# A two-block transformer kernel: the first attention's exponentials read their scores head by head from PSUM, norm offsets move to GpSimd, pair starts are loaded at once, and the work gets a new order

## The reference, cut to what matters

```python
x = x + xattn0(layernorm(x), ctx)     # 16 heads of 16 features, softmax over 77 keys
x = x + ffn0(layernorm(x))            # 256 -> 1024, relu, 1024 -> 256, add its input, layernorm again
x = x + xattn1(layernorm(x), ctx)     # one head; both sides normed
x = x + ffn1(layernorm(x))            # each position takes one of 8 256x256 matrices

scores = einsum('bqhd,bkhd->bhqk', q, k) / 4
weights = softmax(scores, axis=-1)
out = einsum('bhqk,bkhd->bqhd', weights, v)
```

## Time and profile before

| | |
|---|---|
| median of 3 runs | 317.99 us (317.55 to 318.81) |
| span of the profiled execution, first to last instruction | 314.0 us |
| what the runs have around that span (median minus span) | 4.0 us |
| PE busy | 267.9 us (85%) |
| PEld busy | 232.0 us (74%) |
| VectorE busy | 254.8 us (81%) |
| ScalarE busy | 181.7 us (58%) |
| GpSimd busy | 157.3 us (50%) |
| mean granted TensorE clock | 0.932 of full speed |

### The profile page before, as it was taken

The page is one execution under the profiler, slowest core; times in us unless marked ns, Lnnn a source line. Parts: engine busy times, 40 slices in busy tenths (PEclk is TensorE's granted clock), DMA queues, the critical chain, the costliest instruction groups (busy, mean ns, idle before and its releaser), DMA issues.

```text
span 314.0 us, 6283 instructions
## 1 busy us (share of the span) xinstructions
PE 267.9 (85%) x2080; PEld 232.0 (74%) x2080; DVE 254.8 (81%) x664; ACT 181.7 (58%) x606; POOL 157.3 (50%) x157
## 2 busy tenths in 40 slices
PE   2954958977999998999999989999989999878960
PEld 2743937763999698689789959988878988666850
DVE  2998998972889999998997789899899986875640
ACT  2468628526368857478695857775754471454510
POOL 2253640275225878821652263268766653164854
PEclk9995596995999999999999999999999999997995
DMA  6922010240000372100001000011110000000222
GB/s 177 336 72 77 8 42 25 67 142 27 3 0 3 115 222 51 29 24 2 2 0 35 2 0 2 33 52 51 37 36 0 2 0 1 3 0 34 87 78 73
DMA packets 8797, 15.32 MB, mean 49 GB/s; under 512 B 1270, under 2 KB 6813, under 8 KB 8509
## 3 DMA queue, kind: packets, MB, share of 16 engines
q1 hardware_dynamic: 6845, 9.68, 9.2%
q0 software_dynamic: 1920, 5.25, 5.9%
HBM read 11.77 MB, written 3.15 MB: 48 GB/s over the span
## 4 chain that ended last, share of the span: by engine, by line
PE 37%; DVE 29%; issue 15%; POOL 12%; ACT 3%; DVEq 1%; DMA 1%; POOLq 0%; SPq 0%; ACTq 0%
PE PB L256 16%; PE PB L249 7%; PE PB L460 5%; DVE SM L598 3%; POOL SM L1220 3%; DVE SX L649 3%; DVE SM L609 3%; PE S L365 3%; PE S L377 2%; POOL out_x L1282 2%; DVE WD L837 2%; PE PB L327 2%; POOL RAW L1275 2%; DVE XN L701 2%; POOL HL L1254 2%
## 5 line engine op out<-in xcount | busy, mean ns | idle before, releaser
L1220 POOL TENSOR_TENSOR SM<-SM,nhalf 128x2 f32<-128x2 f32 x40 | 29.4, 737 | 98.4 <-DVE SM L604 97.9
L1060 ACT ACTIVATE E<-S,SX 128x77 f32<-128x77 f32 x128 | 39.5, 340 | 16.8 <-DVE SX L652 16.6
L256 PE MATMUL PB<-XTH,W1H 128*128 128x256 f32 x128 | 38.3, 299 | 3.9 <-issue 2.2
L1254 POOL TENSOR_TENSOR HL<-HF,HH 128x512 fp32r<-128x512 f32 x26 | 34.5, 1335 | 13.6 <-DVE HH L682 12.0
L1094 ACT ACTIVATE HF<-PB,cols 128x256 f32<-128x256 f32 x64 | 26.8, 473 | 20.9 <-PE PB L256 20.6
L256 PE MATMUL PB<-W2H,HH 128*128 128x256 f32 x128 | 37.9, 296 | 1.1 <-DVE HL L688 1.1
L256 PE MATMUL PB<-XTH,W1L 128*128 128x256 f32 x128 | 36.4, 284 | 0.0
L256 PE MATMUL PB<-XTL,W1H 128*128 128x256 f32 x128 | 36.4, 284 | 0.0
L256 PE MATMUL PB<-W2H,HL 128*128 128x256 f32 x128 | 35.8, 280 | 0.0
L256 PE MATMUL PB<-W2L,HH 128*128 128x256 f32 x128 | 35.8, 279 | 0.0
L460 PE MATMUL PB<-WD,XP 128*128 x120 | 29.9, 402 | 0.8 <-issue 0.8
(11 more groups left out here) (188 smaller groups left out, 778.3 us busy)
## 6 DMA issues: line engine op xcount, KB each, us to landing
RAW<-in_w SPq DMA_DIRECT2D x4, 512.0 KB, 5.0
WD<-in_WD SPq DMA_DIRECT2D x2, 1024.0 KB
X<-in_x SPq DMA_DIRECT2D x4, 256.0 KB, 7.1
x<-X SPq DMA_DIRECT2D x4, 256.0 KB, 2.2
bc<-in_rows SPq DMA_DIRECT2D x1, 768.0 KB, 7.3
RAW<-in_w_q SPq DMA_DIRECT2D x1, 256.0 KB, 4.2
Wo<-in_w_o SPq DMA_DIRECT2D x1, 256.0 KB, 7.8
RAW<-in_WqT SPq DMA_DIRECT2D x1, 256.0 KB
```

Source lines behind the costliest of these rows:

```text
L256: t = e.matmul(dst, a, b, start=first and j == 0, stop=last and j == n - 1)
L1060: t = e.activation(Ei[:, h * NK:(h + 1) * NK], P[:, at:at + NK], ACT.Exp, bias=SX[:, i, 2, k:k + 1], accum_out=SX[:, i, 1, k:k + 1])
L1220: e.tensor_tensor(sm(K, g, 9), sm(K, g, 8), nhalf[:, :], ALU.pow).then_inc(s["rs" + K], 1)
L1254: e.tensor_tensor(HL[:, hs, :], HF[:, (4 * g + j) % 3, :, :], f(HH[:, hs, :]), ALU.subtract).then_inc(s["hlP"], 1)
```

## The change

- Every `(g, i, a)` of the first attention now takes the by-head path: 8 exponentials from PSUM with sums. The subtraction, the sum and the separate negation on VectorE are gone; the maximum is written negated (`negate=True`) by the reduction itself. The PSUM area is let go when the exponentials are done, in all cases. `smax` now waits for the exponentials of the group before instead of for its transposes, and `ssum` for its `rr`.
- `rs` on GpSimd makes, besides the inverse root, -mean (a product with a tile of -1) and -mean/deviation, in two more instructions of 128x2 with a wait between; line 609 on VectorE is gone.
- The 15 beginnings are read in one call on each of PE, VectorE and ScalarE (`starts()`), at a fixed place in the middle of the first attention.
- The lists of all four engines are written anew. Stage C of groups 0 to 4 comes later (`cs(0)` now stands behind `w1(4, ...)` and before `w1(5, ...)` on PE), `q` and `sc` of group 0 earlier.

The diff, cut to its core (the new lists are told by the rows below and by two of their lines):

```diff
+        minus = sb("minus", [128, 2])
...
+        def load_starts(e, row, most, at):
+
+            values = nc.values_load_multi_w_load_instructions(EV[0:1, row, 0:NP], engines=[e.engine],
+                                                              min_val=0, max_val=most)[1]
+            for n in range(NP):
+                at[n] = values[n]
...
-                P = hold(("sc", g, i, a), ("S", k), ("ex", n + 1) if by_head(i, a) else ("sub", n // 2 + 1))
+                P = hold(("sc", g, i, a), ("S", k), ("ex", n + 1))
...
+            def starts():
+                w.wait_ge(s["route2"], 1)
+                load_starts(e, 0, 7 * 256, start)
...
-                    if n not in start:
-                        start[n] = e.value_load(EV[0:1, 0, n:n + 1], min_val=0, max_val=7 * 256)
...
-                e.scalar_tensor_tensor(out=sm(K, g, 10), in0=sm(K, g, 6), scalar=-1.0, in1=sm(K, g, 9),
-                                       op0=ALU.mult, op1=ALU.mult).then_inc(s["mr" + K], 1)
...
             def smax(g, i, a):
-                n, sv, mx_, hs = scores(g, i, a)
                 w.wait_ge(s["sc"], n + 1)
                 if g:
+                    w.wait_ge(s["ex"], n - 3)
+                e.tensor_reduce(two(SX[:, i, 0, 8 * a:8 * a + 8]), sv, AX, ALU.max, negate=True).then_inc(s["mx"], 1)
+
+            def ssum(g, i, a):
+                n, hs = 4 * g + 2 * i + a, slice(8 * a, 8 * a + 8)
+                w.wait_ge(s["ex"], n + 1)
+                if g:
                     w.wait_ge(s["rr"], n - 3)
-                    w.wait_ge(s["tE"], n - 3)
-                step(e.tensor_reduce(mx_, sv, AX, ALU.max))
-                settle()
-                if by_head(i, a):
-                    e.tensor_scalar(SX[:, i, 2, hs], SX[:, i, 0, hs], -1.0, None, ALU.mult).then_inc(s["neg"], 1)
-                else:
-                    e.tensor_tensor(E[:, i, a, 0:8 * NK].rearrange("p (u h k) -> p u h k", u=2, h=4), sv,
-                                    mx_.unsqueeze(3).to_broadcast([128, 2, 4, NK]),
-                                    ALU.subtract).then_inc(s["sub"], 1)
...
                 e.reciprocal(SX[:, i, 2, hs], SX[:, i, 1, hs]).then_inc(s["rc"], 1)
...
-                if by_head(i, a):
-                    P = bank("sc", g, i, a)
-                    w.wait_ge(s["neg"], n // 2 + 1)
-                    if g:
-                        w.wait_ge(s["tE"], n - 3)
-                    for h in range(8):
...
-                else:
-                    w.wait_ge(s["sub"], n // 2 + 1)
-                    t = e.activation(Ei, Ei, ACT.Exp)
+                P = bank("sc", g, i, a)
+                w.wait_ge(s["mx"], n + 1)
+                if g:
+                    w.wait_ge(s["tE"], n - 3)
+                for h in range(8):
+                    at = h // 4 * 512 + h % 4 * NK
+                    k = 8 * a + h
+                    t = e.activation(E[:, i, a, h * NK:(h + 1) * NK], P[:, at:at + NK], ACT.Exp,
+                                     bias=SX[:, i, 0, k:k + 1], accum_out=SX[:, i, 1, k:k + 1])
...
                 e.tensor_tensor(sm(K, g, 9), sm(K, g, 8), nhalf[:, :], ALU.pow).then_inc(s["rs" + K], 1)
+                if K != "Y":
+                    e.tensor_tensor(sm(K, g, 11), sm(K, g, 6), minus[:, :], ALU.mult).then_inc(s["nm"], 1)
+                    minus_made[0] += 1
+                    w.wait_ge(s["rs" + K], g + 1)
+                    w.wait_ge(s["nm"], minus_made[0])
+                    e.tensor_tensor(sm(K, g, 10), sm(K, g, 11), sm(K, g, 9), ALU.mult).then_inc(s["mr" + K], 1)
...
+            w2(6, 1, 0); tB(7, 2); w2(6, 1, 1); tC(5, 0); cp(4, 1); w1(7, 0, 2); w1(7, 1, 0); cs(5, 2); w1(7, 2, 3)
+            tD(0, 0); co(4); w1(7, 3, 3); pr(0, 0, 0); tD(1, 3); pr(0, 1, 1); w2(7, 0, 0, 3); w2(7, 0, 1); tD(2, 2)
```

More of the change, by code:

```diff
@@ L378, in tE, with pv @@
                 t.then_inc(s["tE"], 1)
-            def pv(g, a, p):
+            def pv(g, a, p=None):
                 w.wait_ge(s["vb"], g // 4 + 1)
                 w.wait_ge(s["et"], 4 * g + 2 + a + 1)
-                P = hold(("pv", g), ("B", p), ("o", g + 1)) if a == 0 else PB[p]
+                P = hold(("pv", g), ("B", p), ("o", g + 1)) if a == 0 else PB[place["pv", g][1]]
                 for c in range(2):
@@ L416, in w2 @@
                     hl_here(w, g, j)
-                P = hold(("w2", g), ("B", p), ("y", g + 1)) if i + h == 0 else PB[p]
+                P = hold(("w2", g), ("B", p), ("y", g + 1)) if i + h == 0 else PB[place["w2", g][1]]
                 ts = slice(i * 128, (i + 1) * 128)
@@ L572, in setup @@
                 step(e.memset(nhalf[:, :], -0.5))
+                step(e.memset(minus[:, :], -1.0))
                 step(e.memset(E[:, :, :, 8 * NK:5 * CW], 0.0))
@@ L737, in vector, with starts @@
             begin = {}
+            def starts():
+                w.wait_ge(s["route2"], 1)
+                load_starts(e, 1, 7 * 256, begin)
             def pa(b, r):
@@ new lines, in vector @@
+            stats("C", 2); ssum(5, 0, 0); hh(3, 0); smax(5, 0, 1); hh(3, 2); ssum(5, 0, 1); o(4); hh(3, 3)
+            smax(5, 1, 0); smax(5, 1, 1); ql(7); x1(4); stats("B", 4); ssum(5, 1, 0); apply("B", 4); ssum(5, 1, 1)
+            lo("B", 4); y(3); stats("Y", 3); o(5); x2(3); hh(4, 0); x1(5); stats("B", 5); apply("B", 5); hh(4, 2)
+            smax(6, 0, 0); hh(4, 3); lo("B", 5); smax(6, 0, 1); apply("C", 1); f_o(); ssum(6, 0, 0); cm(0)
+            ssum(6, 0, 1); stats("C", 3); smax(6, 1, 0); smax(6, 1, 1); cm(1); apply("C", 2); x3_(0); ssum(6, 1, 0)
@@ new lines, in vector @@
+            ssum(6, 1, 1); hh(5, 0); hh(5, 2); y(4); stats("Y", 4); hh(5, 3); o(6); smax(7, 0, 0); smax(7, 0, 1)
+            x2(4); cm(2); ssum(7, 0, 0); apply("C", 3); smax(7, 1, 0); ssum(7, 0, 1); x1(6); smax(7, 1, 1)
+            stats("C", 4); x3_(1); stats("B", 6); y(5); apply("B", 6); stats("Y", 5); ssum(7, 1, 0); ssum(7, 1, 1)
+            lo("B", 6); x3_(2); cm(3); x2(5); hh(6, 0); apply("C", 4); hlD(6, 1); x3_(3); hh(6, 2); stats("C", 5)
+            hh(6, 3); o(7); hlD(6, 3); cm(4); x1(7); stats("B", 7); apply("B", 7); apply("C", 5); stats("D", 0)
@@ L996, in scalar @@
+            apply("D", 7); pa(1, 0); pa(1, 1); pa(1, 2); pa(1, 3); pa(1, 4); pa(1, 5); pa(1, 6); pa(1, 7)
         def scalar(e):
@@ new lines, in scalar @@
+            ex(0, 0, 0); hi("A", 1); ex(0, 0, 1); ex(0, 1, 0); rr(0, 0, 0); rr(0, 0, 1); qh(1); ex(0, 1, 1)
+            rr(0, 1, 0); et(0, 0, 0); apply("A", 2); et(0, 0, 1); w_hi(3); et(0, 1, 0); rr(0, 1, 1); w_hi(4)
+            ex(1, 0, 0); et(0, 1, 1); hi("A", 2); apply("A", 3); ex(1, 0, 1); ex(1, 1, 0); rr(1, 0, 0); rr(1, 0, 1)
+            qh(2); et(1, 0, 0); rr(1, 1, 0); f_ct(); hi("A", 3); et(1, 0, 1); apply("B", 0); hi("B", 0); ex(1, 1, 1)
+            ex(2, 0, 0); hf(0, 0); hf(0, 1); apply("A", 4); rr(1, 1, 1); qh(3); et(1, 1, 0); hf(0, 2); et(1, 1, 1)
@@ L1177, in gpsimd @@
+            pc(0, 7); xtc(7); cpt(6); apply("D", 4); cex(7); apply("D", 5); xtd(4); cpt(7); pc(1, 0); xtd(5); pc(1, 1)
+            apply("D", 6); xtd(6); pc(1, 2); apply("D", 7); xtd(7); pc(1, 3); pc(1, 4); pc(1, 5); pc(1, 6); pc(1, 7)
         def gpsimd(e):
```

236 lines of the change are left out of this document (96 added, 140 removed).

## The result

The changed kernel takes 299.75 us (median of 4 runs, 297.38 to 301.69), the one before 317.77 beside it (4 runs, 315.01 to 318.81): ratio 0.9483, 95% interval [0.9401, 0.9565]. The profiled execution took 301.69 us, its span is 299.9, so 1.8 us lie around the span. In every run of the two kernels whose span is on record these are 1.7 to 2.0 us; the 4.0 us that were worked out for the kernel before joined a median and a span of different executions.

What follows compares the result with a forecast made beforehand. PE (85% busy) and VectorE (81%) were taken to share the bound. Early -8, middle -6, stop +3 and late reads -2 gave -13 us on the 314.0 us span: 301.0, plus 4.0 around it, 305.0 us; range 295 to 321.

Steps and rivals of the forecast that it cites:

- the late part: Sorted stage with its pair products: nothing counted for the new lists, 2 us saved by reading pair beginnings earlier.
- the late reads: Pair beginnings no longer read one by one late in the kernel: 2 us saved, bounds 0 to 10.
- Loads: Busy time over the whole kernel: VectorE falls from 254.8 to 208.8 us, ScalarE rises from 181.7 to 208.6.
- the two links that were to get shorter: ScalarE's waits for VectorE: 12.9 us for offsets and 16.6 us for negated maxima, both expected to shorten.
- Early part: 6 to 80 us: less VectorE work and earlier first exponentials save 8 us, bounds 0 to 16.
- stop: Middle of first attention: PE, ScalarE and VectorE each halt for the single read, about 4.8 us; 3 us on the path.
- Middle: 80 to 280 us: a quarter of PE's 23 us of bubbles goes, 6 us saved, bounds 0 and 23.
- 0.955 of each stretch: Sign for 80 to 280 us: PE's weight-load busy share (PEld) should move nearer the densest old stretch's 0.955.
- The offsets: 64 small products added on GpSimd, 0.33 us each, 21 us in all, hidden under its waits for variances; counted zero.
- ScalarE in VectorE's place: Rival, chance 0.20: ScalarE becomes what is late from 80 to 280 us, which gains nothing; 311 us.
- The sorted stage: Rival, chance 0.18: first fetch of sorted tokens 8 us late, and everything behind it; 323 us, slower.
- The lock: Rival, chance 0.12: GpSimd's offsets hold up VectorE through exclusive SBUF access and give the gain back; 318 us.

## Why the prediction came out right, and which step was wrong

The time (299.75 against 305.0, range 295 to 321) and the sign are right, and so is most of the early and middle part. The step that failed is the late part: the prediction let the new lists cost nothing there and put the late reads at -2. Luck has a part in the closeness, since in the late part two errors of some 9 us nearly cancel. The 4.0 us around the span should have been 1.8, so that the forecast of the span, 301.0, was closer (299.9) than that of the time.

*Loads: right.* VectorE 209.8 us (208.8 was worked out), ScalarE 209.3 (208.6). Eight exponentials take 21.54 - 19.12 = 2.42 us (2.41):

```profile
19.12 0.33 ACT L1046 ACTIVATE E<-S,SX 128x77 f32<-128x77 f32 x1 [1.32 <-DVE SX L645]
21.54 0.64 ACT L1025 ACTIVATE XTH<-PB 128x512 fp32r<-128x512 f32 x1
```

A negated maximum costs 791 ns, a plain one 788. The first exponential is at 19.12 us, 2.1 sooner than the earlier trace rows and not 3. The 10.1 us of stalls in VectorE's offsets did not all vanish: the variance step and `apply` took over about 4, with means of 263 ns (226 before) and 543 (462).

```profile
L608 DVE TENSOR_SCALAR SM<-SM 128x2 f32<-128x2 f32 x40 | 10.5, 263 | 1.4
L621 DVE TENSOR_SCALAR XN<-X,SM 128x256 f32<-128x256 f32 x32 | 17.4, 543 | 7.9 <-POOL SM L1205 5.4 <-PE PB L331 2.2
```

Of the two links that were to get shorter, only one did. ScalarE waits 4.0 us instead of 16.6 for maxima, but 15.0 instead of 12.9 for offsets, now from GpSimd:

```profile
ACT XN L1017 <- POOL SM L1211: 15.0, 10, 4.1
ACT E L1046 <- DVE SX L645: 4.0, 6, 1.3
```

*Early part and stop, -8 + 3: -8.9 measured.* The stop was longer than the 4.8 us estimated, 6.2 on PE (66.9 to 73.1), but for 3.0 us of the gap PE would have waited for `HL`. The early gain itself is near 11: 8.9 and the stop's 2.1, or by the version without the stop (55.70 - 46.07) / 0.89 = 10.8. It lay inside the bounds of 0 to 16.

*Middle, -6: -5.2 measured.* From 80 to 200 us PEld rose from 103.30 to 107.89 us. It did not come near 0.955 of each stretch, though, since the densest stretch itself has 0.907 in the new order: the measure is not the same in two orders.

*The late part: the wrong step.* "PE's queue runs ahead of its matmuls and is idle just 2.3 of the last full 20 us, so I take 2 us saved": this looked at PE's reads and PE's idle time in the old order. In the old order that is about right (PE idles 0.8 us before pair products, and reads at once alone are slower by 1.3%). But ScalarE's and VectorE's reads stand ahead of `XP` and `X`, and in the new order, with reads in place, PE idles 11.4 us before its pair products. The lists tell the likely reason: PE's turn of the first sorted tile stands two calls ahead of its pair products in the new one (`tD(0, 0); co(4); w1(7, 3, 3); pr(0, 0, 0)`) and some two dozen calls ahead in the old one, and ScalarE's copies `XTE` and `XP` with their reads fall between the two. No run changed this distance alone. By the loads, then, the late part with reads in place is some 9 us longer than before, which the sum had at 0, and the reads at once save some 9 there, which it had at 2. Net of their stop the reads are worth 5 to 8 us, where +1 was forecast.

*Hence two errors that cancel.* By stretches: -11 early, +2 stop, -5 middle, +9 late by the new lists, -9 by the reads, together -14 of measured -14.1. By parts: with the reads worth 5 to 8 us of it, exponentials, offsets and lists together bring 6 to 9, where -14 was forecast. They bring them together only: by head alone costs 6.5%, the lists without it bring 0.2%, all of it 5%. The prediction's sum by stretches could not tell that; it wrote that the path "is as long as before" and counted the vanished VectorE turns as gain, and the longer hold of the score area only as a rival for the middle. The runs in the old order show that there this rival's mechanism outweighs the relief.

*The offsets: covered, but each is shorter than estimated.* The two products take 0.19 and 0.22 us (means; 0.33 each estimated), 13.0 us in all where 21 were taken, and by themselves they gain 0.8% in the old order:

```profile
L1211 POOL TENSOR_TENSOR SM<-SM 128x2 f32<-128x2 f32 x32 | 6.9, 215 | 4.9 <-POOL SM L1207 0.5
L1207 POOL TENSOR_TENSOR SM<-SM,minus 128x2 f32<-128x2 f32 x32 | 6.1, 192 | 0.0
```

*The rivals.* ScalarE in VectorE's place: some signs are there in the new order (VectorE's reciprocals wait 9.9 us for exponentials), but the middle gained 5.2 us where this rival has nothing. In the old order it is what happens.

The sorted stage: PE has 2.6 us of waits before pair products, 1.6 of them in one place at 238.74 us; the last fetch begins at 231.3 us (232.3 before) and the pair products begin some 20 us sooner than before, so the fetches are not late by 8. The lock of the Trainium skill (SBUF — State Buffer, "SBUF: two separate sides"): the trace agrees in kind, by the two long instructions beside GpSimd's rests above, though in the kernel before VectorE's product stood still through three products of GpSimd in a row and not through one. Offsets on GpSimd alone gained, so they do not give the time back. Why the offsets' short products hold up so little was not settled.

## What to carry to other kernels

Moving work from the engine that is full to one that has room changes when a shared buffer comes free, and that can be worth more than the load: here the same edit took about 5% off or put 6.5% on, by the order around it. Ask for each edit who waits for the buffer, not only who is busy. Register reads counted here on the engines that feed the bound one: find them by who is waited for in the stage where they stand, in the order in which they will run, which is not the order of the profile at hand. When a stop is placed, put it where the engine would wait anyway, and read the wait that is late next; and a total that comes out right says little about its terms until each was undone by itself.

## What the runs showed of the hardware

One read of 15 values is longer than one of a single value: 1.76 us on PE, 1.64 on ScalarE, 1.80 on VectorE, where single reads took 0.30, 0.28 and 0.30. Behind it each value costs two steps, 0.30, 0.23 and 0.28 us for each value by the first and last start (72.9 - 68.7 over 14, for PE):

```profile
L232 PEldq FUSED_REGOPS  x15: 146/146/165, 68.7 to 72.9; - x15
L232 DVEq FUSED_REGOPS  x15: 183/183/206, 74.8 to 78.7; - x15
L232 PEldq TENSOR_LOAD <-EV x1: 1763/1763/1763, 66.9 to 66.9; - x1
L232 ACTq TENSOR_LOAD <-EV x1: 1641/1641/1641, 68.0 to 68.0; - x1
L232 DVEq TENSOR_LOAD <-EV x1: 1798/1798/1798, 72.9 to 72.9; - x1
```

That is (1.76 - 0.30) / 14 = 0.10 us for each further value. An exponential of 77 columns with its sum takes 0.33 us and the read of the sum 0.19, but they overlap, and the next begins 0.30 us behind:

```profile
19.35 0.19 ACT L1046 ACTIVATION_READ_ACCUMULATOR E<-S,SX 128x1 f32 x1
19.44 0.32 ACT L1046 ACTIVATE E<-S,SX 128x77 f32<-128x77 f32 x1
19.74 0.32 ACT L1046 ACTIVATE E<-S,SX 128x77 f32<-128x77 f32 x1
```
